# Scan stage: another timetable for keys and values, output projections, silu of z, logarithms, residual scaling and row statistics

## The reference, cut to what matters

```python
x = x + mamba(layernorm(x))          # this stage, with the keys and values of the next
x = x + xattn(ctx, ctx, layernorm(x), mask)
x = x + ffn(layernorm(x))

def mamba(residual):                 # per batch row: L=224, D_INNER=1024, D_STATE=16
    hidden = rmsnorm(residual) * norm_w
    x, z = split(hidden @ W_in)      # 2 x 1024
    x = silu(causal_conv4(x) + conv_b)
    dt_r, B, C = split(x @ W_x)      # 64, 16, 16
    dt = softplus(dt_r @ W_dt + b_dt)
    h[t] = exp(dt[t] * A) * h[t-1] + (dt[t] * x[t]) * B[t]
    y = (h . C) + x * D
    return residual + (y * silu(z)) @ W_out
```

## Time and profile before

| | us |
| --- | --- |
| median of 3 runs | 3791.92 |
| lowest, highest | 3791.16, 3794.51 |
| profiled execution | 3798.45 |
| its span | 3797.1 |
| scan stage: first scan of slot 0, last of slot 511 | 123.99, 2092.69 |
| mean granted clock of PE, share of full speed | 0.941 |

### The profile page before, as it was taken

The page is one execution under the profiler, slowest core; times in us unless marked ns, Lnnn a source line. Parts: engine busy times, 40 slices in busy tenths (PEclk is TensorE's granted clock), DMA queues, the critical chain, the costliest instruction groups (busy, mean ns, idle before and its releaser), DMA issues. The chain is left out here.

```text
span 3797.1 us, 59547 instructions
## 1 busy us (share of the span) xinstructions
PE 3285.4 (87%) x20864; PEld 2275.3 (60%) x20864; DVE 2676.5 (70%) x4681; ACT 2390.6 (63%) x5276; POOL 1774.6 (47%) x1052
## 2 busy tenths in 40 slices
PE   4788888888888888888877599999999999969999
PEld 4566556655665556555644366666666666558887
DVE  2698889888988898889889376667667666522321
ACT  4767776778677777777765267666666666522222
POOL 1577777777777777777788000000000000035554
PEclk8899999999999999999988799999999999989999
DMA  3767656765676557655744313122112112021010
GB/s 108 193 166 188 173 130 161 184 173 132 162 190 166 142 150 191 167 143 146 190 131 110 118 33 98 44 61 68 44 50 79 43 50 80 6 76 45 23 45 23
DMA packets 286440, 425.14 MB, mean 112 GB/s; under 512 B 28641, under 2 KB 226273, under 8 KB 281538
## 3 DMA queue, kind: packets, MB, share of 16 engines
q1 hardware_dynamic: 273920, 410.75, 40.3%
q10 hardware_dynamic: 12226, 10.59, 1.0%
HBM read 320.25 MB, written 101.02 MB: 111 GB/s over the span
## 5 line engine op out<-in xcount | busy, mean ns | idle before, releaser
L654 POOL TENSOR_TENSOR a_hs<-a_rep,a_bmat 128x896 f32<-128x896 f32 x512 | 1061.3, 2093 | 358.8 <-PE a_yps L234 323.5
L343 ACT ACTIVATE a_states<-a_rep,a_a_neg 128x224 f32<-128x224 f32 x2048 | 796.5, 438 | 291.1 <-DVE a_hs L568 287.2
L561 DVE TENSOR_TENSOR_SCAN a_states<-a_states,a_hs 128x900 f32<-128x900 f32 x384 | 779.6, 2030 | 164.3 <-ACT a_states L343 163.3
L1164 DVE CUSTOM_DVE_ANT_0 b_sc<-b_sps,b_mask 112x375 f32<-112x375 f32 x1024 | 500.4, 545 | 144.4 <-PE b_sps L975 144.2
L991 PEld LDWEIGHTS b_tps<-b_ident,b_sc 112*125 112x125 f32 x3072 | 401.7, 191 | 279.9 <-issue 142.6
L991 PE MATMUL b_tps<-b_ident,b_sc 112*125 112x112 f32 x3072 | 491.5, 289 | 71.4 <-ACT b_sc L1082 46.1
L1257 POOL TENSOR_TENSOR b_xt<-b_xt,b_bo 112x512 f32<-112x512 f32 x32 | 40.8, 1297 | 1071.2 <-DVE b_ln L1141 1071.2
L1082 ACT ACTIVATE b_sc<-b_sc,b_nmax 112x750 f32<-112x750 f32 x512 | 468.3, 916 | 52.0 <-DVE b_nmax L1170 52.0
L256 PE MATMUL a_work<-a_hT,w_in 128*128 128x224 f32 x2048 | 420.6, 360 | 35.3 <-issue 31.4
L304 PE MATMUL a_work<-wv,ctx 128*125 128x512 f32 x768 | 403.6, 674 | 44.3 <-ACT kv_out L386 38.7
L256 PEld LDWEIGHTS a_work<-a_hT,w_in 128*128 128x128 f32 x2048 | 389.9, 193 | 80.2 <-issue 72.6
(11 more groups left out here) (143 smaller groups left out, 4957.7 us busy)
## 6 DMA issues: line engine op xcount, KB each, us to landing
a_rep<-du_scratch SPq DMA_DIRECT2D x512, 224.0 KB, 6.0
w_in<-W_in_dram SPq DMA_DIRECT2D x128, 512.0 KB, 7.3
du_scratch<-a_du SPq DMA_DIRECT2D x16, 1792.0 KB, 10.9
ctx<-ctxT_dram SPq DMA_DIRECT2D x48, 500.0 KB, 5.0
v_scratch<-kv_out SPq DMA_DIRECT2D x96, 250.0 KB
k_scratch<-kv_out SPq DMA_DIRECT2D x96, 250.0 KB, 2.9
b_keys<-k_scratch SPq DMA_DIRECT2D x16, 1500.0 KB, 11.6
b_v<-v_scratch SPq DMA_DIRECT2D x16, 1500.0 KB
```

The source lines that it names most:

```text
L343: e = act.activation(rows(states[:, g % DA, :])[:, q, 1:ROW], rep[tile % REPS][:, j, 0, :], ACT.Exp, scale=a_neg[:, g % SLOTS, q:q + 1])
L561: dve.tensor_tensor_scan(state if g % G4 else whole, state, whole, 0.0, ALU.mult, ALU.add).then_inc(S["scan"], 1)
L654: pool.tensor_tensor(hs[g % RING][:, :, 1:ROW], rep[tile % REPS][:, j, 1, :].unsqueeze(1).broadcast_to([P, Q, L]), bmat[b % 2][:], ALU.mul ...
L1164: dve.tensor_tensor_reduce(out=sc[block % 2][:, j, cols], in0=sps[0:TT, j, 0:HALF], in1=mask[:, block % 2, cols], scale=-1.0, scalar=3.0e3 ...
```

## The change

Nothing is computed otherwise; instructions move within the engines' programs.

- Keys and values: `KV_SLOTS` of before had slots 8, 10, 12, 14, 18, 22, 26, 28, 30 behind its first three; now 9, 12, 16, 18, 20, 22, 24, 26, 31. Copies, stores and context loads follow.
- Output projections: slots 7 and 10 instead of 7 and 9, their residual sums 9 and 12.
- The silu of z: ACT's slot 15 instead of 10. Logarithms: 6, 8, 10, 12 instead of 5, 7, 9, 11.
- `normalise`: slot 11 instead of 12, and only h; the residual is scaled by `scale_residual` in slot 29. `gains` on POOL two slots earlier.
- Row statistics of the result: out of `add_residual`, both halves together in slot 16 (`x1_stats`); the store waits for the sums alone and stands in slot 13.
- `sum_piece`: slots 8 and 24 instead of 15 and 31.

```diff
--- before.py
+++ after.py
@@ -125,7 +125,8 @@
     KC = 125
     CHUNKS = t["ctxT"].shape[2] // KC
     WIDE = 2 * KC
-    KV_SLOTS = (1, 3, 5, 8, 10, 12, 14, 18, 22, 26, 28, 30)
+    KV_SLOTS = (1, 3, 5, 9, 12, 16, 18, 20, 22, 24, 26, 31)
+    O_SLOTS = (39, 42)
     UNITS = len(KV_SLOTS)
     OUTS = len(shared.kv_out)
     assert TT <= P and 2 * L <= BANK and R + 2 * N <= P and CHUNK <= 2 * BANK and R == 64 and DG == 32
@@ -323,8 +324,8 @@
                         x_dbl(b)
                     if -24 <= lead < -24 + 2 * PAIRS and lead % 2 == 0:
                         dt_raw(b, (lead + 24) // 2)
-                    if at in (SLOTS + 7, SLOTS + 9):
-                        out_proj(b, (at - SLOTS - 7) // 2)
+                    if at in O_SLOTS:
+                        out_proj(b, O_SLOTS.index(at))
                     if at in KV_SLOTS:
                         project_kv(b, KV_SLOTS.index(at))
 
@@ -357,6 +358,8 @@
                 for i in range(2):
                     act.activation(h[:, i, :], xt[b % XS][:, i, :], ACT.Identity, scale=rsqrt[:, 1, i:i + 1],
                                    bias=gain[:, 0, i:i + 1]).then_inc(S["h"], 1)
+
+            def scale_residual(b):
                 act.wait_ge(S["h"], 2 * (b + 1))
                 for i in range(2):
                     e = act.activation(xt[b % XS][:, i, :], xt[b % XS][:, i, :], ACT.Identity, scale=gain[:, 1, i:i + 1],
@@ -487,8 +490,10 @@
                     lead = at + EARLY
                     if lead == -52:
                         guess_rsqrt(b)
-                    if lead == -46:
+                    if lead == -47:
                         normalise(b)
+                    if lead == -29:
+                        scale_residual(b)
                     if lead == -44:
                         keep_hT(b)
                     if -42 <= lead < -42 + 4 * PAIRS and (lead + 42) % 4 == 0:
@@ -501,15 +506,15 @@
                         keep_xd(b)
                     if -23 <= lead < -23 + 2 * PAIRS and lead % 2:
                         softplus_parts(b, (lead + 23) // 2)
-                    if -21 <= lead < -21 + 2 * PAIRS and lead % 2:
-                        softplus_log(b, (lead + 21) // 2)
-                    if lead == -16:
+                    if -20 <= lead < -20 + 2 * PAIRS and lead % 2 == 0:
+                        softplus_log(b, (lead + 20) // 2)
+                    if lead == -11:
                         silus_z(b)
                     if lead in (-14, -13):
                         skip(b, lead + 14)
                     if at - 1 in KV_SLOTS:
                         keep_kv(b, KV_SLOTS.index(at - 1))
-                if slot >= 0 and slot // every < len(pieces) and slot % every == every - 1:
+                if slot >= 0 and slot // every < len(pieces) and slot % every == every // 2:
                     sum_piece(slot // every)
 
         def vector_program():
@@ -582,10 +587,17 @@
                 dve.wait_ge(S["res"], b + 1)
                 dve.tensor_tensor(xt[b % XS][:, i, :], xt[b % XS][:, i, :], work[0:TT, bank, :],
                                   ALU.add).then_inc(S["sum"], 1)
-                dve.wait_ge(S["sum"], 2 * b + i + 1)
-                steps.after(dve.bn_stats(stats1[:, i, :], xt[b % XS][:, i, :]))
+
+            def x1_stats(b):
+                dve.wait_ge(S["sum"], 2 * (b + 1))
+                if b:
+                    dve.wait_ge(S["x1"], b)
+                for i in range(2):
+                    steps.after(dve.bn_stats(stats1[:, i, :], xt[b % XS][:, i, :]))
                 steps.settle()
-                dve.bn_aggr(mv1[:, 2 * b + i, :], stats1[:, i, :]).then_inc(S["x1"], 1)
+                for i in range(2):
+                    e = dve.bn_aggr(mv1[:, 2 * b + i, :], stats1[:, i, :])
+                e.then_inc(S["x1"], 1)
 
             dve.memset(series_bias[:], -(3.0 ** 0.5) / 4.0).then_inc(S["const"], 1)
             dve.memset(log_small[:], LOG1P_SMALL).then_inc(S["const"], 1)
@@ -615,8 +627,10 @@
                         older_taps(b, (lead + 41) // 4)
                     if -22 <= lead < -22 + 2 * PAIRS and lead % 2 == 0:
                         softplus_series(b, (lead + 22) // 2)
-                    if at in (SLOTS + 9, SLOTS + 11):
-                        add_residual(b, (at - SLOTS - 9) // 2)
+                    if at - 2 in O_SLOTS:
+                        add_residual(b, O_SLOTS.index(at - 2))
+                    if at == SLOTS + 16:
+                        x1_stats(b)
 
         def gpsimd_program():
             steps = Steps(pool, S["pool_step"])
@@ -688,7 +702,7 @@
                     lead = at + EARLY
                     if lead == -54:
                         squares_of(b)
-                    if lead == -46:
+                    if lead == -48:
                         gains(b)
                     if lead == -12:
                         softplus_sum(b)
@@ -702,6 +716,7 @@
             def load_x(b):
                 if b >= XS:
                     sp.wait_ge(S[f"xout{b % XS}"], 16 * (b // XS))
+                    sp.wait_ge(S["x1"], b - XS + 1)
                 sp.dma_start(xt[b % XS][:], t["x"][b].rearrange("(i p) d -> p i d", p=TT)).then_inc(S[f"xin{b % XS}"], 16)
 
             def store_bc(b):
@@ -739,7 +754,7 @@
                 spread(b, N, cmat)
 
             def store_x1(b):
-                sp.wait_ge(S["x1"], 2 * (b + 1))
+                sp.wait_ge(S["sum"], 2 * (b + 1))
                 sp.dma_start(x1_dram[b].rearrange("(i p) d -> p i d", p=TT), xt[b % XS][:]).then_inc(S[f"xout{b % XS}"], 16)
 
             def load_piece(n):
@@ -790,7 +805,7 @@
                         spread_bc(b)
                     if lead == -9:
                         store_du(b)
-                    if at == SLOTS + 11:
+                    if at == SLOTS + 13:
                         store_x1(b)
                     if -46 <= lead < -46 + 4 * PAIRS and (lead + 46) % 4 == 0:
                         load_w_in(b, "x", (lead + 46) // 4)
```

## The result

The changed kernel takes 3685.97 us (3681.7 to 3694.06, 4 runs) where the kernel before took 3791.54 beside it (3789.91 to 3794.51, 4 runs): a ratio of 0.9723, 95% interval 0.9705 to 0.9741. That is 105.6 us faster. The forecast was 3718, so its direction and its range held; the gain is 42% larger than the 74 us that the sum gave.

The account below looks back on a forecast made before the run. VectorE (DVE) bounds the scan: 110.9 us of own work a batch plus waits, falling from 15.3 to 10.6, so 121.5. Gains of 54, 5, 9 and 6 us, together 74, off the median 3791.92 give 3718 us; range 3680 to 3765.

Parts of the forecast that it names:

- the sum: Whole kernel: gains of 54 us in 13 batches, 5, 9 and 6 elsewhere, together 74 us.
- The first half: Slots 0 to 15 of a batch: near 56 us (68 before), the waits of slots 10 and 11 gone.
- the prediction's own sign: DVE's waits under 1.5 us in all in slots 10 to 15, and near 1.0 in slot 1.
- The second half: Slots 16 to 31 of a batch: near 65 us (58 before); PE sets the pace and starts late.
- 2.5 us of half clock behind an idle of 5 us: PE from slot 16's sum of states on: starts late and at half clock, 2.5 us taken, bound 3.1.
- the 1.1 us more in slot 17: DVE's add in slot 17 needs the late sum of states: 1.1 us of wait beyond 2.0.
- A: PE isn't slowed in slot 16, late chain 2.5 us shorter: 119.0 us a batch, 3685 us; chance 0.14.
- B: Three groups in PE's second half each a microsecond longer: 124.5 us a batch, 3757 us; chance 0.16.
- C: w_in loads late beside more stores in slots 16 to 27: slower, 3822 us at 8 us a batch; chance 0.06.
- D: GpSimd's chain or PE's order around slot 9 sets the batch, gains return in slots 16 to 20: about 3790; chance 0.04.
- The start and the end: Gains outside the 13 batches: 6 us before the first scan, batch 0 5, batch 14 9, last batch and tail 0.
- The table loads: ACT's silu of z in slot 15: 4.4 us without the skill's drain of 1.38 us a switch.

## Why the prediction was right, and where it was not

*What bounds the kernel.* Right: DVE's own work is 110.5 us a batch (110.9 said), and the batch is that plus its waits. The change is worth what it takes from the waits, 15.3 to 8.4.

*The first half.* Right: slots 0 to 15 take 57.2 us (56 said, 68.1 before). Slot 1 waits 1.21 (1.0 said), slot 9 1.35 (1.6), slots 12 and 14 0.67 and 0.17 (0.5 and 0.2), slots 10 and 11 nothing. One wait was missed: 1.76 in slot 15 (0.4 said). ACT copies the values of slot 12 ahead of the skip, at 764.29, and waits 1.39 us for PE to end them; I had counted ACT's load in that slot and not what the copy waits for. By the prediction's own sign (under 1.5 us of waits in all in slots 10 to 15) this half isn't quite as said: they are 2.6. Yet the wait of 1.76 cost nothing, as the values in slot 13 showed.

*The second half: the step that failed.* I said 65 us and it is 61.7 (58.2 before). Two facts of it held: PE needs 14.73 us for each group of four slots (14.7 said) and runs without idle from slot 16 to 27, and GpSimd's chain takes 16 us from the last logarithm to the product (760.10 to 776.05). What failed is the term *2.5 us of half clock behind an idle of 5 us* and with it the 1.1 us more in slot 17. I laid the slow stretch behind the sum of states, in series with PE's 44.2 us. It fell on the x projection ahead of the sum, beside GpSimd's chain. (With the values in slot 13 it does fall on the sum and the keys behind it, and costs 2.7 us there.) And the chain is timed from slot 12, so that the missed wait of 1.76 brings its end nearer to slot 16: 5.25 us, not 6.5. Together PE starts its run 3.75 us less late. In DVE's waits that is slot 17 2.24 instead of 3.1, slot 21 none instead of 1.9, slot 25 0.46 instead of 1.3. By term: waits 8.4 instead of 10.6, DVE's own work 0.4 less, and 0.4 a batch for the batches of 117.3 us, below, and the shorter last one; these 3.0 us by 13 batches are the 39 us by which batches 1 to 13 were missed.

*The rivals.* A gave 119.0 a batch and 3685 us, which are the numbers measured. Its mechanism, that half clock costs nothing there, is what happened, though not because PE isn't slowed: it is slowed where nobody waits for it. That its 119.0 is met to the tenth is luck: the first half's waits are 1.5 us more than said, the second half's 3.6 less. B (three heavier groups) and C (loads of w_in late) fall: between slots 16 and 27 PE has no idle, ahead of projections or elsewhere. D falls as a whole. But its reason, that a gain in slots 10 to 15 comes back in 16 to 20, is what the experiments with half of the change show: so it goes with the silu back, and with the values in slot 13.

*The start and the end.* The first scan came 3.8 us sooner (6 said), batch 0 gained 1.7 (5 said). Why less, no run tells, and the spread of the first scans, 5 us, is about what is missing. Batch 14 gained 6.9 of 9.

*The table loads.* The load takes 1.28 us and the next activation starts 1.29 behind its start, in the new place too (770.67 and 771.96): the whole silu, with both loads, takes 4.4 us. The Trainium skill ("ScalarE: Activation LUTs", What ACT_TABLE_LOAD costs) has a drain of 1.38 us on top of each switch. By that, as an estimate, slot 17 would wait twice 1.38 longer, 5 us; it waits 2.24. (Over 13 batches that would be 36 us, where the prediction has 37.) The measurement decides: no drain here.

*What I had not asked.* The sum priced the parts against the rest of the new kernel, which is right for the whole, and says nothing on one part alone. Alone, the new slots of keys and values lose 34 us; with all else new, the old slots lose some 110. Neither came near what was expected of it, in size or, for the first, in sign.

## What to carry to other kernels

With engines that work in order, a copy that waits is paid by everything queued behind it: place each unit of filler work so that its matmuls end before the engine that copies them gets there, and look first at what the neighbour in the same slot is. A wait of the bounding engine is only worth removing if no other chain ends at the same place; take the time from a fixed starting event (here the last logarithm) to the next meeting point, and see whether the faster engine would arrive early. Where several moves are made at once, a price worked out for one is a price in that company alone.

## What the hardware showed that I had not expected

The first output projection stands behind an idle of PE of 2.88 us in nearly all kernels that keep its place, with the same 16 matmuls, and takes 7.12, 8.82 or some 10 us (8.72 to 8.82 behind an idle of 1.95 with the weight sum back). Which of them it is doesn't look random: before it is 8.82 in most batches; in the change 8.82, with 7.12 in three of the 13; with half of the keys and values 10.05 and 8.62 in the first two and 7.12 in all others; the same with the silu in slot 16, 8.82 in all; with the unit in slot 28, 9.98 in five in a row. In both kernels with half of the keys and values PE starts the values (3.7 us), the dt (0.92) and this projection at the same 16.22, 19.75 and 23.56 us behind slot 0's scan, so its work right ahead of the idle is not what differs. Two batches of the change; the second is 117.2 us long, the first 119.0:

```profile
501.04 8.82 PE L285 MATMUL a_work<-a_w_out,a_yT 128*112 128x512 f32 x16 [2.88 <-DVE a_du L556]
620.02 7.12 PE L285 MATMUL a_work<-a_w_out,a_yT 128*112 128x512 f32 x16 [2.88 <-DVE a_du L556]
```

In the 4 us from 738, under such an 8.82, the granted clock is 0.58; in the 4 us from 620, under the 7.12, it is 1.00:

```profile
738.00:742.00 4.00, 4.00 (x6) 0.58 0.78 200
620.00:624.00 4.00, 3.98 (x10) 1.00 0.84 217
```

So an idle of this length sometimes brings the lower of the two levels (1.2 GHz) and sometimes not, and how long it stays differs. In some kernels the outcome repeats from batch to batch, and then it looks like a property of the kernel: two kernels with the same period of 116.0 us keep to 7.12 and to 8.82. In others it changes with no change of the period ahead of it, as in the change, where batches of 119.0 us come before each of 117.2. Its price is a wait of 1.35 or 2.5 us a batch in DVE's slot 9, 18 or 33 us over 13 batches, that an unrelated edit seems to turn on or off; there is one traced execution of each kernel. The Trainium skill ("TensorE: Matmul & The Clock Gate", What's actually happening) says that the number of slow matmuls at a kernel's start varies with the gate's phase, and puts the cost of that start under 1% of a kernel. The batches here show such a variation within one execution; 18 or 33 us are 0.5 or 0.9% of this kernel, under that figure too, though as much as the single edits above were to bring. What decides the outcome wasn't tried.
